# First FFN of a two-layer gated block: first-layer products once per group, cycles combined per token

## The reference

```python
x = x + tanh(g_xattn[0]) * L0_xattn(layernorm(x), ctx)        # stage A: norm, product, decayed scan, pick
x = x + tanh(g_ffn[0])   * L0_ffn(layernorm(x))               # stage B, below
x = x + tanh(g_xattn[1]) * L1_xattn(ctx, layernorm(x), mask)  # stage C: masked attention, 8 heads
x = x + tanh(g_ffn[1])   * L1_ffn(layernorm(x))               # stage D: low-rank FFN

def twist(x):
    o_r, o_i, p_r, p_i = split(x, 4, axis=-1)
    return concatenate([p_r, -p_i, -o_r, o_i], axis=-1)

def L0_ffn(x):
    gf = global_net(x.mean(axis=1, keepdims=True))            # one number per batch
    out = x
    for _ in range(3):
        h = gelu(out @ w1 + b1)                               # 256 -> 256
        h = gelu(h @ w2 + b2)                                 # 256 -> 128
        h = gelu(h @ w3 + b3)                                 # 128 -> 64
        tf = sigmoid(h @ w4 + b4)                             # 64 -> 1
        coupling = 0.1 + adaptive_range * (0.7 * gf + 0.3 * tf - 0.5) * 2
        out = out + coupling * twist(out)
    return out
```

## Time and profile before

| | |
|---|---|
| median of 3 runs | 687.62 us (687.56 to 689.57) |
| the profiled execution | 689.92 us |
| its span | 687.1 us |
| granted clock over the span | 0.99 of full |
| PE busy | 644.9 us, 94% of the span |
| ACT busy | 434.3 us, 63% |
| DVE busy | 430.2 us, 63% |
| POOL busy | 202.5 us, 29% |

### The profile page before, as it was taken

How to read it: one execution, slowest core, us unless ns; L and a number is a source line. 1 busy time by engine, 2 the same in 40 slices (tenths; PEclk the granted TensorE clock), 3 DMA queues, 4 the chain that set the end, 5 groups by cost and what they waited for, 6 DMA issues and landing times.

```text
span 687.1 us, 11443 instructions
## 1 busy us (share of the span) xinstructions
PE 644.9 (94%) x3490; PEld 440.5 (64%) x3490; DVE 430.2 (63%) x982; ACT 434.3 (63%) x1164; POOL 202.5 (29%) x299
## 2 busy tenths in 40 slices
PE   4988899999999998699999999999999987899997
PEld 2764555555544457588877878888888865656654
DVE  7974758786775748376666666666666686152522
ACT  7666655535544433577777778777787777545452
POOL 6575423310110012124443333333332220142110
PEclk9999999999999999899999999999999999899999
DMA  8821116401000005534434544444444440001112
GB/s 283 258 78 62 60 33 245 96 1 62 0 1 0 1 0 126 127 78 110 107 89 118 125 115 105 107 109 107 100 103 124 93 94 3 1 14 50 53 40 92
DMA packets 43124, 57.88 MB, mean 84 GB/s; under 512 B 6118, under 2 KB 25926, under 8 KB 42950
## 3 DMA queue, kind: packets, MB, share of 16 engines
q1 hardware_dynamic: 43078, 57.33, 30.4%
HBM read 27.46 MB, written 4.19 MB: 46 GB/s over the span
## 4 chain that ended last, share of the span: by engine, by line
PE 75%; SPq 8%; DMA 4%; DVE 4%; ACT 3%; issue 3%; POOL 2%; DVEq 0%; POOLq 0%; ACTq 0%
PE bank L1134 12%; SPq L504 7%; PE bank L1420 6%; PE bank L1146 6%; PE bank L1331 6%; PE bank L1350 6%; PE bank L1396 4%; PE bank L1556 4%; PE bank L1373 4%; PE bank L1359 4%; PE bank L1110 3%; PE bank L1413 3%; PE bank L1546 3%; DMA c_stack<-neg_row 2%; PE bank L1114 2%
## 5 line engine op out<-in xcount | busy, mean ns | idle before, releaser
L931 ACT ACTIVATE c_junk<-bank,c_nmx 128x256 bf16<-128x256 f32 x256 | 117.5, 486 | 15.7 <-DVE c_nmx L1883 15.5
L1883 DVE TENSOR_REDUCE c_nmx<-bank 128x4 f32<-128x1024 f32 x64 | 75.4, 1219 | 36.9 <-PE bank L1373 36.9
L1134 PE MATMUL bank<-b_o,cw 128*128 128x512 f32 x192 | 90.6, 603 | 1.8 <-ACT b_o L795 1.8
L953 ACT ACTIVATE c_pT<-bank 128x1024 f32<-128x1024 f32 x64 | 61.7, 1014 | 5.9 <-PE bank L1396 5.6
L771 ACT ACTIVATE b_h<-bank,cols 128x512 f32<-128x512 f32 x48 | 32.9, 687 | 51.0 <-PE bank L1134 50.8
L1042 ACT ACTIVATE d_h<-bank,cols 128x512 f32<-128x512 f32 x64 | 39.7, 686 | 39.3 <-PE bank L1547 39.3
L1134 PEld LDWEIGHTS bank<-b_o,cw 128*128 128x128 f32 x192 | 34.5, 190 | 44.9 <-issue 41.1
L1331 PE MATMUL bank<-c_ctxT,wsrcT 128*128 128x256 f32 x256 | 61.8, 386 | 0.4 <-DVE c_vb L1875 0.4
L1350 PE MATMUL bank<-wsrcT,c_ctxT 128*128 128x256 f32 x240 | 56.7, 379 | 0.0
L1396 PE MATMUL bank<-c_stack 99*128 99x256 f32 x256 | 48.4, 322 | 8.6 <-DMA c_stack<-c_rows 8.2
L931 ACT ACTIVATION_READ_ACCUMULATOR c_junk<-bank,c_nmx 128x1 f32 x256 | 55.8, 218 | 0.0
(11 more groups left out here) (184 smaller groups left out, 1298.3 us busy)
## 6 DMA issues: line engine op xcount, KB each, us to landing
c_stack<-c_parts SPq DMA_DIRECT2D x192, 128.0 KB
a_ctx<-in_ctx SPq DMA_DIRECT2D x16, 512.0 KB, 3.9
c_ctxT<-in_ctx_turned SPq DMA_DIRECT2D x16, 512.0 KB, 3.6
out_x<-x_sb SPq DMA_DIRECT2D x7, 512.0 KB, 2.9
x_sb<-in_x SPq DMA_DIRECT2D x3, 1024.0 KB, 9.5
mask_b<-in_mask SPq DMA_DIRECT2D x1, 2048.0 KB, 11.9
x_sb<-in_x SPq DMA_DIRECT2D x2, 512.0 KB, 5.6
wsrcT<-in_w_src_turned SPq DMA_DIRECT2D x1, 1024.0 KB, 7.0
```

The costliest lines, as they stand in the source:

```text
L931: op = nc.scalar.activation(c_junk[:, tc, j, :], scores(tc)[:, j, :], ACT.Exp, bias=c_nmx[hg][:, tc, j:j + 1], accum_out=c_sum[hg][:, tc, ...
L953: nc.scalar.activation(c_pT[hg][:, :, q * S:(q + 1) * S], scores(q), ACT.Exp).then_inc(c_pT_ok, 1)
L1134: op = mm(bank[2 * u + h][:], cw1[:, c, h * P:(h + 1) * P], b_o[n % LANES][:, c, :], start=c == 0, stop=c == DK - 1)
L1883: v.tensor_reduce(c_nmx[hg][:, tc, :], scores(tc), AXIS.X, ALU.max, negate=True)\
```

## The change

The kernel before takes layer 1 anew in each of three cycles. In the new one, `first_b` takes the four products of `x` with `cw1` and four of `x` with `cw1t`, a copy of the weights with rows exchanged and signed (made by two DVE operations in `constants_b`), once per group. For cycle 1 ACT makes the gelu from the first four and copies them to `b_s`; it copies the other four to `b_r` (`second_b`). For cycles 2 and 3 DVE combines `b_s` and `b_r` with the coupling of each token (`first_state_b`, `second_state_b`: two coupling operations and two of 1024 columns each), POOL brings the pair `b_s`, `b_r` on by one cycle (`twisted_b`, two of 1024 columns), and ACT makes the gelus from SBUF (`hidden_b`, behind a copy that stacks the couplings, `stacked_b`). Layers 2, 3 and 4 are done per item; layers 3 and 4 are folded on 256 columns.

The state itself is no longer turned back. PE turns the three stacked couplings into token columns (`columns_b`, four tiny products), DVE brings them into shape, POOL works out three factors per token in ten small operations (`factors_b`), and DVE adds to `x` from the normalised rows `b_xn`, now kept in four buffers (`x_b`: four operations of 256 columns and eight of 128, all from SBUF). `back_b` is gone.

A slot `g` now holds the third cycle of group `g - 2`, the second of `g - 1` and the first of `g`; the global net is done per group. The table of units begins one unit later, and in slot 0 a turn and a mix stand ahead of the first products. Behind the slots the last items of groups 6 and 7 are mixed with the first products of stage C. The x updates of groups 6 and 7 stand inside the first pass of `body_c` on DVE; `factors_b` of group 6 stands at the end of POOL's last slot, that of group 7 behind `split_k(1)`.

The core of the diff, in this order: the table; POOL's functions and slot; ACT's; PE's, with what follows its slots; DVE's.

```diff
-UNITS = ((2, 3, 4, 5), (6, 7, 8), (9, 10), (11, 12), (13, 14), (15,))
+UNITS = ((3, 4, 5), (6, 7, 8), (9, 10), (11, 12), (13, 14), (15,))
...
+            def twisted_b(n):
+                s, r = b_s[n % LANES], b_r[n % LANES]
+                pool.wait_ge(b_s2, n + 1)
+                nc.gpsimd.tensor_tensor(s[:], s[:], b_tt[0][:].unsqueeze(1).to_broadcast([P, DK, GROUP]), ALU.mult)\
+                    .then_inc(b_rmid, 1)
+                pool.wait_ge(b_rmid, n + 1)
+                nc.gpsimd.tensor_tensor(r[:], r[:], s[:], ALU.subtract).then_inc(b_r2, 1)
...
+            def factors_b(n):
+                s = n % 2
+                c = [b_cc[s][:, :, k] for k in range(CYCLES)]
+                gate = gates[:, 1:2]
+                pool.wait_ge(b_cc_ok, n + 1)
+                need(pool, b_x2, n - 1)
+                nc.gpsimd.tensor_tensor(b_mul[:], c[0], c[1], ALU.mult)
+                nc.gpsimd.tensor_tensor(b_b2[:], c[0], c[1], ALU.add).then_inc(b_chain, 1)
...
+            def slot_b(g):
+                units = units_at(g)
+                for b in units[:-1]:
+                    unit_a(b)
+                if 0 <= g - 1 < NG:
+                    twisted_b(g - 1)
+                for b in units[-1:]:
+                    unit_a(b)
+                if 0 <= g - 3 < NG // 2:
+                    stats_b(g - 3)
+                if 0 <= g - 2 < NG:
+                    factors_b(g - 2)
...
             split_k(1)
+            factors_b(NG - 1)
             over_batches(pool, body_c)
...
+            def hidden_b(n, c):
+                stacked_b(n, c - 1)
+                act.wait_ge((b_s2, b_s3)[c - 1], n + 1)
+                if n > 0:
+                    act.wait_ge(b_ps[1], ITEM[n - 1, c] + 1)
+                src = (b_t, b_s)[c - 1][n % LANES]
+                for h in range(DK):
+                    nc.scalar.activation(b_h1[c][:, h, :], src[:, h, :], ACT.Gelu, bias=cb1[:, h:h + 1])\
+                        .then_inc(b_h_ok[c], 1)
...
+            def slot_b(g):
+                units = units_at(g)
+                first, second, third = (0 <= g - c < NG for c in range(CYCLES))
+                if g == 0:
+                    squares_a(5)
+                    scaled_a(4)
                     unit_a(units[0])
+                    units = units[1:]
+                if first:
+                    first_b(g, 0)
+                if third:
+                    layer2_b(g - 2, 2)
+                if first:
+                    first_b(g, 1)
+                if third:
+                    layer3_b(g - 2, 2)
+                    layer4_b(g - 2, 2)
+                if g == NG - 1:
+                    xnTq_c(0, 6)
+                for b in units[:-1] if len(units) > 1 else units:
+                    unit_a(b)
+                if second:
+                    hidden_b(g - 1, 1)
+                    layer2_b(g - 1, 1)
+                global_b(g, 0)
+                second_b(g, 0)
+                if second:
+                    layer3_b(g - 1, 1)
+                global_b(g, 1)
+                second_b(g, 1)
+                if second:
+                    layer4_b(g - 1, 1)
+                layer2_b(g, 0)
                 if len(units) > 1:
+                    unit_a(units[-1])
+                global_b(g, 2)
+                layer3_b(g, 0)
+                if second:
+                    hidden_b(g - 1, 2)
+                if g + 1 < NG:
+                    turned_b(g + 1)
+                layer4_b(g, 0)
...
+            def first_b(n, i):
+                h = i % DK
+                if i == 0:
+                    pe.wait_ge(b_xT_ok, n + 1)
+                if i >= DK:
+                    pe.wait_ge(b_ab_ok, PARTS_B * n + i - 1)
+                    pe.wait_ge(s_vconst, 9)
+                w = (cw1, cw1t)[i // DK]
                 for c in range(DK):
+                    op = mm(bank[h][:], w[:, c, h * P:(h + 1) * P], b_xT[:, c, :], start=c == 0, stop=c == DK - 1)
...
+            def slot_b(g):
+                units = units_at(g)
+                first, second, third = (0 <= g - c < NG for c in range(CYCLES))
+                if g == 0:
                     next_unit()
+                    units = units[1:]
+                first_b(g, 0)
+                if third:
+                    layer2_b(g - 2, 2)
+                first_b(g, 1)
+                if third:
+                    layer3_b(g - 2, 2)
+                if g == NG - 1:
+                    both_free()
+                    xnT_c(0, 0, 6)
+                if third:
+                    layer4_b(g - 2, 2)
+                for b in units[:-1] if len(units) > 1 else units:
+                    next_unit()
+                if second:
+                    layer2_b(g - 1, 1)
+                global_b(g, 0)
+                first_b(g, 2)
+                if second:
+                    layer3_b(g - 1, 1)
+                global_b(g, 1)
+                first_b(g, 3)
+                if second:
+                    layer4_b(g - 1, 1)
+                layer2_b(g, 0)
                 if len(units) > 1:
                     next_unit()
+                global_b(g, 2)
+                layer3_b(g, 0)
+                if third:
+                    columns_b(g - 2)
+                if g + 1 < NG:
+                    turn_b(g + 1)
+                layer4_b(g, 0)
...
+            layer2_b(NG - 2, 2)
             q_c(0, 0, 7)
+            layer3_b(NG - 2, 2)
+            k_c(0, 0, 6, range(0, 1))
+            layer4_b(NG - 2, 2)
+            layer2_b(NG - 1, 1)
+            k_c(0, 0, 6, range(1, DK))
+            layer3_b(NG - 1, 1)
+            columns_b(NG - 2)
+            layer4_b(NG - 1, 1)
+            pe.wait_ge(b_ab_ok, PARTS_B * NG)
+            k_c(1, 1, 0)
+            pe.wait_ge(c_q_ok, 1)
+            xnT_c(1, 1, 7)
+            v_c(0, 0, 0, 1)
+            layer2_b(NG - 1, 2)
+            v_c(0, 0, 1, 1)
+            layer3_b(NG - 1, 2)
+            layer4_b(NG - 1, 2)
+            columns_b(NG - 1)
...
+            def first_state_b(n):
+                s, r, t = b_s[n % LANES], b_r[n % LANES], b_t[n % LANES]
+                couplings_b(n, 0)
+                dve.wait_ge(b_ab_ok, PARTS_B * (n + 1))
+                need(dve, b_h_ok[1], 2 * (n - LANES + 1))
+                v.tensor_tensor(t[:], r[:], b_tt[0][:].unsqueeze(1).to_broadcast([P, DK, GROUP]), ALU.mult)\
+                    .then_inc(b_mid, 1)
+                dve.wait_ge(b_mid, 2 * n + 1)
+                v.tensor_tensor(t[:], t[:], s[:], ALU.add).then_inc(b_s2, 1)
...
             def x_b(n):
-                dve.wait_ge(b_back, n + 1)
-                for h in range(2):
-                    xh = rows(GT * n + 2 * h, 2)
-                    op = v.scalar_tensor_tensor(xh, bank[back_banks(n)[h]][:], gates[:, 1:2], xh, ALU.mult, ALU.add)
+                s = n % 2
+                dve.wait_ge(b_fin, n + 1)
+                xn = b_xn[n % XNS]
+                for k in range(GT):
+                    xk = rows(GT * n + k, 1)
+                    op = v.scalar_tensor_tensor(xk, xn[:, k, :], b_ga[s][:, k:k + 1], xk, ALU.mult, ALU.add)
+                op.then_inc(b_xmid, 1)
+                dve.wait_ge(b_xmid, n + 1)
+                for k in range(GT):
+                    to = x_sb[:, GT * n + k, :].rearrange("p (c d) -> p c d", c=4)
+                    of = xn[:, k, :].rearrange("p (c d) -> p c d", c=4)
+                    v.scalar_tensor_tensor(to[:, 0:4:3, :], of[:, 2:0:-1, :], b_gb[s][:, k:k + 1], to[:, 0:4:3, :],
+                                           ALU.mult, ALU.add)
+                    op = v.scalar_tensor_tensor(to[:, 1:3, :], of[:, 3::-3, :], b_gn[s][:, k:k + 1], to[:, 1:3, :],
+                                                ALU.mult, ALU.add)
                 op.then_inc(b_x2, 1)
...
+            def last_slots_b():
+                first_state_b(NG - 1)
+                biased(c_qT, bank[7], bq_col, 0, c_q_ps, c_q_ok, c_qlo_ok, 0)
+                x_b(NG - 3)
+                biased(c_kT, bank[6], bk_col, 0, c_k_ps, c_k_ok, c_k_split, 0)
+                second_state_b(NG - 1)
+                columns_b(NG - 2)
+                biased(c_kT, bank[0], bk_col, 1, c_k_ps, c_k_ok, c_k_split, 2)
+                v_c(0, 1)
+                columns_b(NG - 1)
...
                 if first:
+                    x_b(NG - 2)
                     x_b(NG - 1)```

In the listings of the order of instructions, a row is a line, an operation, what it writes and reads, its output's shape and how often it stands in a row. First PE in a plain slot, before: `b_h1` holds what layer 1 left, `b_h2` layer 2, `b_h3` layer 3, with the pair's lane behind.

```order
L1134 MATMUL bank<-b_o0,cw1 128x512 x4
L1152 MATMUL bank<-b_h20,cw3 64x512
L1152 MATMUL bank<-b_h21,cw3 64x512
L1134 MATMUL bank<-b_o1,cw1 128x512 x2
L1160 MATMUL bank<-b_h3,cw4 128x512 x2
L1134 MATMUL bank<-b_o1,cw1 128x512 x2
L1146 MATMUL bank<-b_h10,cw2 128x512 x2
L1146 MATMUL bank<-b_h11,cw2 128x512 x2
```

648 lines of the change are left out of this document (257 added, 391 removed).

## The result

| | before | after |
|---|---|---|
| median | 687.59 us (4 runs, 684.92 to 689.57) | 720.13 us (4 runs, 719.88 to 720.59) |
| ratio after to before | | 1.0477, interval 1.0441 to 1.0513 |
| the profiled execution, its span | 689.92, 687.1 us | 719.88, 718.1 us |
| granted clock over the span | 0.99 | 0.967 |
| PE busy | 644.9 us, 94% of the span | 637.4 us, 89% |

What follows compares the result with a forecast made beforehand. TensorE alone was taken to bound the first FFN; saved work less new waits, later start and passage put SyncE's first stack transfer 12.6 us later, plus 4 behind it: 16.6 more, 704 us against the 687.62 median, range 688 to 718.

Steps and rivals of the forecast that it cites:

- PE work: First FFN, per group: TensorE work falls from 21.3 to 18.2 us, 25 us less in all.
- The gaps: TensorE waits in the first FFN's slots, where one item's chain has nothing left between: 27.1 us in all.
- A: Plain slot, between layer 3 and layer 4 of the third-cycle item: TensorE waits 1.06 us for ACT.
- C: Plain slot, between layer 2 and layer 3 of the new group: TensorE waits .47 us.
- D: Plain slot's end, before the next slot's first product: chain of 7.1 us against other TensorE work, wait 1.6 us.
- B: Plain slot, between third-cycle layer 4 and second-cycle layer 2: TensorE waits 1.9 us for ACT's tanh, stacking copy and gelu.
- PE's 5.5: At the slot's end: 5.5 us of other TensorE work beside the chain from second-cycle layer 4 to the next first product.
- The clock: Rival: clock falls inside the slots, 4 us of work in each of seven at .50; +28 us, 732; chance .03.
- Start and passage: First product at 41.9 instead of 36.12; last first-cycle layer 4 to SyncE's stack transfer 25.5, then first scores 11.94 later.
- Behind it: After the first scores: x updates of groups 6 and 7 ahead of DVE's first shift cost -1 to 6, taken as 4 us.
- DVE as the bound: Rival: in slots 2 to 5 POOL's long operations hold back DVE, 3.5 us per slot, +14, 718; chance .08.

Runs made afterwards that it cites:

- first experiment on the gaps: Kernel after, with second-cycle hidden gelus ahead of the first products' second half (ACT), that cycle's layer 2 ahead of third-cycle layer 4 (PE): median 705.34 us.
- the last run: Three half products nobody reads fill two waits behind the last slots, against the reordered-slot kernel with later x updates and earlier tanh (685.53 us): median 678.29 us, ratio 0.988.
- the best kernel: The kernel of the last run: new slot order, twisted state on DVE, two waits filled with products nobody reads; median 678.29 us, ratio 0.988 to before.

## Why the size was wrong, by the prediction's own steps

The span grew by 31.0, forecast was 16.6; the missing 14.4 are in the places below. Put by cause, PE work makes 8.3 of them, and rows at the low clock some 6: 1.4 at the start, 1.7 and 1.3 in slots 6 and 7, 1.7 in the passage to stage C (an estimate: these rows less the same ones at full clock).

**The gaps were right.** Forecast 27.1 in all, measured some 27.4 (the 31.1 in the table hold also 3.2 ahead of slot 0). A 1.06 and 1.05; C .47 and .47; D 1.6 and 1.48 (1.03 and 2.37 in slots 0 and 1); B 1.9 and, in the two slots without a unit, 2.14 and 2.75. That D came so close is in part luck: the terms named for PE's 5.5 there add up to 5.1, without the small global step; in slot 5 PE's part, with C, took 5.97 (202.47 to 208.44) and the chain 7.45 instead of 7.1, two errors that cancel. The first experiment on the gaps showed that A and B come from the order; closing D showed the next wait.

**PE work was the step that failed.** The plain slot's work was put at 18.2; read from slot 5 with its unit left out it is 19.3, at clock 1.00. The seven rows of two products each last 1.72 to 1.92 up to the next row and come to 12.8, not 12.2: I had priced all 14 at .87, the pace inside a run of eight, though most here stand beside another shape, for which the same group had a price (1.92). Five of the seven take 1.81 to 1.92, the layer 2 at 186.32 and 195.31 take 1.72; where four products stand together in this kernel too (44.29), they take 3.43 up to the next row, 1.72 for two. The columns take .91 (estimated .7), the entering transposes 1.00 (.88), and layers 4 and the global steps .1 more each. So slots 0 to 5 are .6 to 1.4 longer each than forecast (6.1 together), all with one sign. For slots 6 and 7 the same error makes 2.2. So the saving on PE, put at 25, was nearer 17.

**The clock was left out of the sum.** It stood as a rival of its own with 4 us in each of seven slots. It came in part: in slots 6 and 7, at the start and behind the stage. Slots 6 and 7 are 3.1 and 3.2 longer than forecast, 4.0 more than the error of work explains; the two long rows alone are 1.7 and 1.3 of it, and the run with the filled gap B confirmed the cause for these rows. Between 60 and 200, where units fill the slots, the clock was 1.00 throughout, so as a rival for the whole stage it fell. The Trainium skill, "TensorE: Matmul & The Clock Gate", section "Part 1: The HAM clock gate", calls the throttled level the default and lets activity release it; the rows at 219.80 and 246.68 agree in kind, and the 140 us at 1.00 with PE 88% busy show that an emptier PE need not pay.

**Start and passage.** The first product came 2.4 later than the 41.9 forecast: the scaled rows started at 38.01 instead of 37.08 (POOL's chain for them began .4 later, and one operation of it took .72 instead of .19 beside VectorE's new twisting of the weights, which I had not costed), and the turn and mix behind the 6.12 of idleness took 5.14 instead of 3.7, with the clock at .51 from 39.15 to 42.56. From kernel to kernel this turn starts up to 1.4 earlier or .8 later, so a part of the .9 is scatter. From the last first-cycle layer 4 (260.56) to SyncE it took 27.7, not 25.5, again with a row at low clock (3.59 at 261.06). From there to the first scores 12.00 against 11.94.

**Behind it** the term was 4, measured 1.3 net. The first transposed scores come 35.1 later, which is 5.4 more than the first scores, but later batches give most of it back, as before had small waits there that after has not. Together: 2.4 + 12.4 (slots) + 2.2 + .1 - 2.7 = 14.4.

**DVE as the bound** did not happen: at D PE waits for ACT. The hold-up that fed this rival is real. In the kernel after, the four operations of the x update took 5.85 beside POOL's two of 2.4 to 2.5, and 1.66 without, 4.2 lost where 5.1 was priced; in the run with the twisted state on DVE they take 1.66 in the slots too (the last row):

```profile
213.67 5.85 DVE L1807 SCALAR_TENSOR_TENSOR x_sb<-b_xn,b_ga,x_sb 128x256 f32<-128x256 f32 x4
...
312.63 1.66 DVE L1807 SCALAR_TENSOR_TENSOR x_sb<-b_xn,b_ga,x_sb 128x256 f32<-128x256 f32 x4
```

```profile
185.28 1.66 DVE L1807 SCALAR_TENSOR_TENSOR x_sb<-b_xn,b_ga,x_sb 128x256 f32<-128x256 f32 x4
```

The rule of the Trainium skill, "SBUF — State Buffer", section "Who interferes with whom", agrees, for these operations have two SBUF inputs. The hold-up was hidden (DVE idles 4.71 ahead of the second state at 229.57), and came out as soon as D was closed.

**What stays open.** Whether the order of small steps makes it likelier that the clock falls, why it fell behind 2.14 in slot 6 and not behind 2.37 ahead of slot 2, how much of the last run's gain is the clock at the passage to stage D, and, in the best kernel, the 5.38 that PE still waits for the rows of the shift. That neighbours of another shape are what makes the products slower is read from rows; no run varied it, and the layer 2 at 195.31 is at full pace between two other shapes.

## What to carry to other kernels

Work that is saved on the bounding engine counts only if the new order still has, between two steps of one item, as much work of others as the item's chain takes on the helper engines; write down each gap, and try to close it by order before giving up the saving. Price a step from a row with the same neighbour, since a wrong pace in every step of a repeated slot adds up with one sign, and the range must move as a whole by it. Where an order leaves waits or gathers small steps, add the products behind them at the lower clock to the sum, not only to a rival, and try whether filling one wait brings the clock back.

## What the runs showed of the hardware that I had not expected

The granted clock differs between executions of one and the same kernel where its waits leave it in doubt: with the columns ahead of layer 3, .961 to .978 and 698.16 to 707.62 us. A few products that nobody reads, put where PE would wait, bought 4 us in the kernel after (medians of two and four executions) and 7 in the best one, with the passage to stage D as an open part of the 7. In one execution the clock fell at a wait of .57 among small steps (122.09 above), while waits of .50 to 2.37 in the kernel after left it at 1.00 from 60 to 200.
